# Relation maps copied in three pieces, ahead of the loop's other transfers

## What is computed

```python
attn_scores = jnp.einsum('bihd,bjhd->bhij', q, k) / scale
li = x @ rel_W[:, :d].T
lj = x @ rel_W[:, d:].T
logits = li[:, :, None, :] + lj[:, None, :, :] + rel_b
relation_probs = jax.nn.softmax(logits, axis=-1)
bias = jnp.einsum('bijk,hk->bhij', relation_probs, logical_bias)
gate = jax.nn.sigmoid(x @ gate_W.T + gate_b)
attn_scores = attn_scores + gate * bias
attn_weights = jax.nn.softmax(attn_scores, axis=-1)
```

## Time and profile before

| | us |
|---|---|
| median of 3 runs | 5007.06 (5003.76 to 5009.56) |
| the profiled execution | 5018.32 |
| its span in the trace | 5016.4 |
| TensorE busy | 4458.2 (89%) |
| DVE busy | 3821.7 (76%) |
| ACT busy | 3380.7 (67%) |
| POOL busy | 2057.0 (41%) |

### The profile page before, as it was taken

The page is one execution under the profiler, slowest core; times in us unless marked ns, Lnnn a source line. Parts: engine busy times, 40 slices in busy tenths (PEclk is TensorE's granted clock), DMA queues, the critical chain, the costliest instruction groups (busy, mean ns, idle before and its releaser), DMA issues. The chain is left out here.

```text
span 5016.4 us, 183232 instructions
## 1 busy us (share of the span) xinstructions
PE 4458.2 (89%) x74128; PEld 3458.1 (69%) x74128; DVE 3821.7 (76%) x6309; ACT 3380.7 (67%) x4458; POOL 2057.0 (41%) x1809
## 2 busy tenths in 40 slices
PE   6459999999999999999999999999999996289992
PEld 3227777777777777777777777777777785267771
DVE  4388888888888888888888888888888843167773
ACT  2017887888787788877877787888888882044440
POOL 0114444444444444444444444444444442433335
PEclk9659999999999999999999999999999998589996
DMA  7514544544555445554454455454554456244434
GB/s 96 82 33 112 118 113 111 118 112 115 113 112 112 111 114 116 113 118 110 114 114 112 109 113 116 113 119 115 115 114 111 112 114 178 79 146 149 150 137 113
DMA packets 496919, 573.65 MB, mean 114 GB/s; under 512 B 136360, under 2 KB 369704, under 8 KB 492096
## 3 DMA queue, kind: packets, MB, share of 16 engines
q1 hardware_dynamic: 486880, 543.96, 46.5%
q0 software_dynamic: 6144, 16.79, 1.1%
q10 hardware_dynamic: 3040, 0.98, 0.1%
HBM read 305.10 MB, written 46.65 MB: 70 GB/s over the span
## 5 line engine op out<-in xcount | busy, mean ns | idle before, releaser
L734 DVE TENSOR_REDUCE b_mxp<-b_mx 128x1 f32<-128x512 f32 x4096 | 2635.4, 686 | 559.0 <-PE b_mx L835 508.9
L703 ACT ACTIVATE b_pr<-b_sc 128x1024 f32<-128x1024 f32 x2048 | 1986.5, 1021 | 697.0 <-PE b_sc L824 689.2
L814 PE MATMUL b_sc<-b_qm,kst 128*128 128x128 f16 x16384 | 1272.3, 220 | 54.3 <-ACT b_pr L703 42.0
L824 PE MATMUL b_sc<-b_cm,b_rst 112*128 112x128 f16 x16384 | 1264.5, 220 | 42.8 <-DMA b_rst<-b_rhi 35.5
L814 PEld LDWEIGHTS b_sc<-b_qm,kst 128*128 128x128 f16 x16384 | 971.6, 98 | 283.7 <-issue 229.5
L860 PE MATMUL b_acc<-b_pr,vp 128*32 128x128 f32 x32768 | 1124.1, 277 | 27.3 <-issue 26.9
L824 PEld LDWEIGHTS b_sc<-b_cm,b_rst 112*128 112x128 f16 x16384 | 1012.0, 98 | 49.4 <-DMA b_rst<-b_rhi 40.4
L860 PEld LDWEIGHTS b_acc<-b_pr,vp 128*32 128x32 f32 x32768 | 839.2, 110 | 265.2 <-ACT b_pr L703 190.2
L636 POOL TENSOR_TENSOR b_ex<-b_ex 128x512 f32<-128x512 f32 x512 | 654.7, 1279 | 680.8 <-ACT b_ex L682 680.8
L835 PE MATMUL b_mx<-kst,b_qx 64*128 64x512 f16 x4096 | 819.4, 397 | 92.1 <-DVE b_mxp L734 76.9
L642 POOL CAST b_rhi<-b_ex 128x512 f16<-128x512 f32 x512 | 312.8, 611 | 1293.0 <-ACT b_ex L690 1244.5
(11 more groups left out here) (144 smaller groups left out, 1726.0 us busy)
## 6 DMA issues: line engine op xcount, KB each, us to landing
b_dj<-key_logits SPq DMA_DIRECT2D x256, 768.0 KB, 7.9
b_rst<-b_rhi SPq DMA_DIRECT2D x2048, 64.0 KB, 3.2
b_rst<-b_rlo SPq DMA_DIRECT2D x1024, 64.0 KB, 3.1
c_w1r<-in_L_ffn_W_dram SPq DMA_DIRECT2D x23, 1024.0 KB, 4.9
c_w2r<-in_L_ffn_W_dram SPq DMA_DIRECT2D x23, 1024.0 KB, 4.8
expert_tokens<-c_zeros SPq DMA_DIRECT2D x23, 512.0 KB, 6.8
c_xb<-expert_tokens SPq DMA_DIRECT2D x23, 512.0 KB
expert_results<-c_y SPq DMA_DIRECT2D x23, 512.0 KB, 2.9
```

The lines of the kernel that those rows point to most:

```text
L703: nc.scalar.activation(pr[:, jt % 2, half, :], sc[:, half].rearrange("p a b -> p (a b)"), ACT.Exp).then_inc(s["p_ready"], 1)
L734: nc.vector.tensor_reduce(mxp[:, head, part:part + 1], mx[:, (bank + ab) % MX_RING, :], AX.X, ALU.max).then_inc(s["mx_used"], 1)
L814: pe.matmul(sc[:, half, side, p * P:p * P + P], kst[:, pair, jt * P:jt * P + P], qm[:, par, :, pair, side * IS:side * IS + IS], start=(p = ...
L824: ins = pe.matmul(out, rst[:, u % 2, b, j0:j0 + P], cm[:, par, half, b], start=False, stop=(b % (NB // 2) == NB // 2 - 1), skip_group_chec ...
```

## The change

Queries are laid over the partitions in another order. Token 8i+b of a tile now lies on partition 16b+i (before: one order for each half of the tile, token 64s+4i+b on partition 64s+16b+i), and `const` for the maps is loaded with the tile's tokens in the order 8i+b. So the 128 rows of a map are in the order of the 16 rows of `b_rst` times 8 blocks, and one copy does what two did for the two sides: three copies for a map, 128 rows each, in the place of six of 64. The constants of the maps take one copy for two. The numbers that the waits count are adapted.

And the loop is written in another order. In each unit all copies of both maps come first, then the key logits (`sp_dj`), and what a unit has beside them comes last; the query parts go from unit 0 to unit 2, the raw-score queries from unit 1 to unit 3. The row bound stays in unit 6.

```diff
 def by_block(tokens):
-    return tokens.rearrange("o (t s i b) d -> (o s) b i t d", s=2, i=BI, b=NB // 2)
+    return tokens.rearrange("o (t i b) d -> (o b) i t d", i=BI, b=NB)
...
         def sp_consts(sp, x, par):
...
-            for side in range(2):
-                sp.dma_start(const[IS * side:IS * side + IS, par, 0:4],
-                             const_dram[bass.ds(x, 1)].rearrange("o (s b i) n -> (o s) i b n", s=2, b=NB // 2)[side, :, :, 0:4]
-                             ).then_inc(s[f"const_in{par}"], 16)
+            sp.dma_start(const[:, par, 0:4],
+                         const_dram[bass.ds(x, 1)].rearrange("o (b i) n -> (o i) b n", b=NB)[:, :, 0:4]).then_inc(s[f"const_in{par}"], 16)
...
         def sp_r(sp, x, u, k):
             sp.wait_ge(s["lo_ready"], 16 * x + 2 * u + k + 1)
             waited(sp)
-            for side in range(2):
-                for part, t in enumerate((rhi, rlo, rhi)):
-                    row = 32 * part + BI * k
-                    sp.dma_start(rst[row:row + BI, u % 2, NB // 2 * side:NB // 2 * side + NB // 2, :],
-                                 t[IS * side:IS * side + IS, 2 * (u % 2) + k, :]).then_inc(s[f"r_in{u % 2}"], 16)
+            for part, t in enumerate((rhi, rlo, rhi)):
+                row = 32 * part + BI * k
+                sp.dma_start(rst[row:row + BI, u % 2], t[:, 2 * (u % 2) + k, :]).then_inc(s[f"r_in{u % 2}"], 16)
...
                     for k in range(2):
                         if u + 1 < UNITS:
                             sp_r(sp, c, u + 1, k)
                         elif not last:
                             sp_r(sp, c + 1, 0, k)
-                        if u == 0 and k == 0 and not last:
-                            sp_q(sp, c + 1, 1 - par)
-                        if u == M_UNIT and not last:
-                            if k == 0:
-                                sp_m_out(sp, c + 1)
-                            else:
-                                sp_m_in(sp, c + 1, 1 - par)
                     if u + 4 < UNITS or not last:
                         sp.wait_ge(s["d_ready"], 32 * c + 4 * u + 12)
                         waited(sp)
                         sp_dj(sp, (u + 4) % UNITS)
                     if u == 1:
                         sp_att(sp, c)
-                        if more:
-                            sp.wait_ge(s["c_made"], 2 * c + 2)
-                            waited(sp)
-                            sp_qx(sp, c + 2, par)
+                    if u == 2 and not last:
+                        sp_q(sp, c + 1, 1 - par)
+                    if u == 3 and more:
+                        sp.wait_ge(s["c_made"], 2 * c + 2)
+                        waited(sp)
+                        sp_qx(sp, c + 2, par)
+                    if u == M_UNIT and not last:
+                        sp_m_out(sp, c + 1)
+                        sp_m_in(sp, c + 1, 1 - par)
                     if u + 1 == UNITS and more:
                         sp_consts(sp, c + 2, par)
...
-                pool.wait_ge(s[f"r_in{u % 2}"], 192 * (UNITS // 2 * x + u // 2))
+                pool.wait_ge(s[f"r_in{u % 2}"], 96 * (UNITS // 2 * x + u // 2))
```

More of the change, by code:

```diff
@@ L190, in _ @@
                     sp.dma_start(x[BI * b:BI * b + BI, 8 * q:8 * q + 8, :],
-                                 by_block(hidden)[b // 4, b % 4, :, 8 * q:8 * q + 8, :]).then_inc(x_in[q], 16)
+                                 by_block(hidden)[b, :, 8 * q:8 * q + 8, :]).then_inc(x_in[q], 16)
             for m in (2, 3, 0, 1):
@@ L717, in dve_d @@
             if g == 0 and n == 0:
-                dve.wait_ge(s[f"const_in{par}"], 48 * nth)
+                dve.wait_ge(s[f"const_in{par}"], 32 * nth)
             if k == 0 and n == 0:
@@ L819, in pe_scores @@
             if jt % 4 == 0 and half == 0:
-                pe.wait_ge(s[f"r_in{u % 2}"], 192 * (UNITS // 2 * c + u // 2 + 1))
+                pe.wait_ge(s[f"r_in{u % 2}"], 96 * (UNITS // 2 * c + u // 2 + 1))
             for b in range(NB):
@@ L1050, in _ @@
                 for b in range(NB):
-                    sp.dma_start(x1[BI * b:BI * b + BI, t, :], by_block(hidden)[b // 4, b % 4, :, t, :]).then_inc(s[f"h_in{q}"], 16)
+                    sp.dma_start(x1[BI * b:BI * b + BI, t, :], by_block(hidden)[b, :, t, :]).then_inc(s[f"h_in{q}"], 16)
             sp.wait_ge(s["zeroed"], 1)
@@ L1073, in _ @@
                 for b in range(NB):
-                    sp.dma_start(by_block(out)[b // 4, b % 4, :, t, :], x1[BI * b:BI * b + BI, t, :]).then_inc(s["stored"], 16)
+                    sp.dma_start(by_block(out)[b, :, t, :], x1[BI * b:BI * b + BI, t, :]).then_inc(s["stored"], 16)
             sp.wait_ge(s["stored"], 16 * NB * GROUPS)
```

## The result

The changed kernel is slower: median 5217.67 us of 4 runs (5208.57 to 5221.45) against 5005.41 of the kernel before, ratio 1.0422, 95% interval [1.0404, 1.044]. The forecast was 5184, range 5105 to 5255. The profiled execution took 5208.57, 190.3 more than that of before.

The account below looks back on a forecast made before the run. TensorE, busy 89%, was taken as the bound, idling for map rows and, through the row-bound chain, for ACT. +177 + 40 - 35.5 - 5 = +177 on 5018.32 gave 5195, less 11.3 for the median 5184; range 5105 to 5255 us.

Parts of the forecast that it names:

- Direction and place: Slower (0.85): in unit 6 the bound's copy waits behind key logits, delaying POOL, then ACT, then TensorE.
- Lateness of L620, 13.3: POOL's start on matrix cm, waiting for the row bound: 13.3 us behind DVE's bound, in the place of 7.6.
- the term of +177: Row bound behind unit 6's key logits: +5.7 us a chunk, 31 times, +177 us.
- The pass from lateness to time: From the bound through POOL and ACT to TensorE: beyond 6.4 us, each us of lateness costs one us.
- Low clock, +40, with -5 for the map rows: TensorE's lower clock after long waits: 1.3 x 31 = +40 us; about -5 from shorter map-row waits.
- Map rows, -35.5: TensorE's waits for b_rst go, as unit 0's last map copy goes out some 7 us earlier: -35.5 us.
- The three copies, nothing beyond their issue: 128-row map copies on SP's queue: 0.6 us an issue, well under a us added to the 3.2 landing.
- the small copy is not held up: Rival: the bound lands in 1.4 us behind key logits too, giving 4973 us; chance 10%.
- key logits pass in half the time on an empty queue: Rival: unit 6's key logits take half of 7.9 us, L626 starts at 9.7, giving 5047 us; chance 6%.
- The map rows' waits didn't stay: Denies the rival that new map copies cost 1.2 us or land late, keeping these waits: 5224 us; chance 8%.
- the delay was not swallowed: Denies the rival that slack in ACT's exponentials absorbs a later L626: near 4970 us or no change; chance 3%.
- Token order, 0 with 5 to both sides: by_block's new stride: stages at both ends could move a few us either way; put at 0, 5 to both sides.

Follow-up runs that it names:

- kernel 1: The changed kernel with the row bound's two copies moved ahead of unit 6's wait for d_ready and key logits: 4998.17 us, ratio 0.9987 to the kernel before.
- kernel 2: The kernel before with only the row bound's two copies moved behind unit 6's key logits: 5198.14 us, ratio 1.0382.
- kernel 9: The changed kernel with the row bound's two copies between unit 6's wait for d_ready and its key logits: 5013.14 us, ratio 1.0025 to the kernel before.
- kernel 4: The kernel before with only the query copies moved, from unit 0 to 2 and from unit 1 to 3: 4948.04 us, ratio 0.9886.
- kernel 3: The kernel before with only the three 128-row copies a map and the new token order, loop order as before: 5019.21 us, ratio 1.0023.
- kernel 7: The kernel before, six copies a map and old token order kept, with the loop order of kernel 1: 4933.87 us, ratio 0.9859.
- kernel 5: The changed kernel with the row bound's copy out issued by ACT on its own queue: 5192.28 us, ratio 1.0364 to the kernel before.
- kernel 6: The changed kernel with the bound's copy out ahead of unit 6's d_ready wait, only the copy back behind the key logits: 5198.68 us, ratio 1.0373 to the kernel before.
- kernel 10: The kernel before with only the bound's copy back moved up, directly behind its copy out, ahead of unit 6's second map: 4978.42 us, ratio 0.9949.
- kernel 8: Kernel 1 with each 128-row copy split in two by columns, 64 KB a copy: 4963.03 us, ratio 0.9927 to the kernel before.
- kernel 11: The kernel before with the moves of kernel 4 and kernel 10 together, six copies a map: 4932.9 us, ratio 0.9854.

## Why the prediction held

*Direction and place.* Right. The bound's copy out is issued 3.8 us behind the bound (3.7 forecast) and lands after 6.8 (6.9 forecast); POOL, ACT and TensorE wait in the order given, in all 31 chunks. Kernels 1, 2 and 9 show that this transfer ahead of the bound makes the loss.

*Lateness of L620, 13.3.* It was 12.5: with nothing more ahead on the queue, the copy back and the start of POOL take 1.8 from issue, not 2.5. So the term of +177 measures 4.9 x 31 = 152, of which the wait for ACT shows +136. The pass from lateness to time, one for one from 6.4 us on, nearly held: (12.5 - 6.4) x 31 is 189, and the wait for ACT 178.

*Low clock, +40, with -5 for the map rows.* Too small: TensorE is busy 58 us longer, 1.9 a chunk. I took one stretch of 3.4 us as in the earlier trace rows for each wait; the clock records show stretches of 6.8 us at the lower level in 28 cases. And the kernel before paid more than "the few chunks" of the prediction, 13 stretches of 3.4.

*Map rows, -35.5.* Right in the waits (-31). But I gave this gain to the copies and the moved queries together, and the experiments part them: moving the queries alone empties these waits (kernel 4), the copies alone take 13.5 of them (kernel 3).

*The three copies, nothing beyond their issue.* This step failed. I asked for the time of their issue (0.6, right) and of their landing (3.2 became 4.5, more than the "well under a us" that I gave it, and harmless) and not who else uses the transfer engines. In the changed kernel TensorE's issue rows grew by 34 us; between kernels 1 and 7, which differ in the copies and the token order, it is 64 us of time.

*How near the sum came is in part luck.* From profiled execution to profiled execution the forecast was +177 and it came to +190. The waits for ACT were 41 less than forecast; against them stand the issue rows (34, put at nothing) and the busy time (58 in the place of 35). The other 20 of the 34 us between 5184 and 5217.67 lie in the step from the profiled execution to the median: I took 11 off, and the changed kernel's profiled execution was its fastest, 9 below its median. The chunks took (4237.6 - 330.0) / 31 = 126.1 us; 125.6 was forecast.

*The rivals.* That the small copy is not held up fell at once (it landed after 6.8). That key logits pass in half the time on an empty queue did as well: in unit 6 they land after 7.1, against 8.4 in the median of all. The map rows' waits didn't stay, and the delay was not swallowed: TensorE waited in all 31 chunks.

*Token order, 0 with 5 to both sides.* The stretches ahead of the first row bound and behind the last are 331.7 and 968.4 us before, 330.0 and 968.9 after. Right.

## What to carry to other kernels

Before a small transfer that somebody waits for is moved on a queue, look at what then stands ahead of it: its price is the drain of that transfer, here 5.4 us a time (6.8 less 1.4) on a chain without slack, and another queue did not avoid it (kernel 5). Take a wait whose loss is one for one with lateness as a chance too: here the same two copies moved the other way gain. And count for a merged transfer not only its issue and its landing but the bytes that one issue puts on the shared engines at once: here the instruction packets go over the same engines, and got slower.

## What the runs showed of the hardware that I had not expected

TensorE's waits without a named cause end 1.15 to 1.85 us behind the arrival of an instruction packet, nearly all of them in every kernel (45 of 50 at the least, in kernel 6), and they sum to 76 to 99 us when the map copies are of 128 KB and to 29 to 57 when they are of 64. A 1 KB packet from 128 rows to 16 takes 96 ns in a copy of 128 KB and 61 in one of 64, at the same 0.6 us of issue. Of the 39 us that TensorE waited for ACT, 26 came back when the wait was taken away (kernel 10).

In kernels 3, 7, 8 and 9 TensorE's wait for DVE's maxima rose from 17 to between 32 and 39 us, in 1, 10 and 11 it did not (19.6, 19.5, 16.8). The lateness of L620 parts the two groups: its mean is 6.1 to 7.1 us in the first and 4.5 to 5.0 in the second. And the added waits lie 16 to 20 us behind the bound, where they sum to 16 to 27 us in the first group and to 2 to 4 in the second. So a lateness near 6.4 us isn't free yet: part of it seems to reach TensorE by way of DVE. By which instructions is not shown.
